# Key projection of the biased attention's first pair moved into the delta stage, and its bias turned through four PSUM banks around the norm

## The chip, the cores and the metric

The kernel runs on one core of a Trainium2 chip, in one launch. The metric is the device time of that launch in microseconds, the median of several runs. The engines are named as the profile names them: PE (matrix engine; PEld is its loading of weights), DVE (vector), ACT (scalar), POOL (GpSimd) and SP, which here only issues DMAs.

## The reference

Two batches of 256 tokens of width 256 go through six stages, each of which adds its result to x:

```
x = x + xattn_0(layernorm(x), ctx, ctx)            # 8 heads, 4096 context rows: "plain"
x = x + delta_rule(layernorm(x))                   # gated delta rule, chunks of 32: "delta"
x = x + experts(layernorm(x))                      # 15 experts, top 3, and a shared one
x = x + xattn_1(layernorm(x), ctx, ctx, bias)      # 16 heads, 4096 context rows: "biased"
x = x + quantised_attention(layernorm(x))
x = x + recurrent_cell(layernorm(x))
```

The biased attention is the stage whose beginning is changed:

```
k = split_heads(ctx @ Wk.T);  v = split_heads(ctx @ Wv.T);  q = split_heads(layernorm(x) @ Wq.T)
scores  = einsum('bhqd,bhkd->bhqk', q, k) * 256 ** -0.5 + bias      # bias is [256, 4096]
weights = softmax(scores);  out = merge_heads(weights @ v) @ Wp.T
```

Its keys depend on the context and a weight only, not on x. All is float32.

## The kernel before

Each stage is one block in which every engine has a program of its own, written out in order; semaphores join them, and the stages follow each other. `c.iterations`, `c.batches` and the semaphores of `c.attention` count on over the stages.

**Attention.** `cross_attention` works on pairs of heads, 8 pairs for each batch row in the biased stage, so 16 sweeps and the one ahead of them. Scores are held with the keys on partitions, in 16 tiles `kp` of 256 keys. While pair m is attended, the scores of pair m+1 are made, and the keys of pair m+2 and the values of pair m+1 are projected in pieces of 512 keys (`PIECES`). The first pair has no sweep ahead of it that could project its keys. At the head of the stage PE therefore runs `first_keys(g)` for eight groups `g` of 512 keys, each two float32 matmuls of 512 columns (line 320), through banks 4 to 7, and ACT copies each to `KT` (line 497).

**Bias.** It comes as queries by keys and has to be turned. `turn_bias(kp)` is four transposes into bank `kp % 3` (line 465), and DVE copies the bank back into `BIAS` (line 661). PE's order is: keys 0 and 1, the eight transposes of the normed x (line 128), a wait for their copy (`ln_ready`, DVE line 120), the queries (line 347), and then for g from 2 to 7 keys g and three `turn_bias`. The first scores (line 369) wait for the last copy.

**Norm.** DVE takes moments (lines 95, 98), ACT a square root (line 104), DVE the inverse and the normed rows (lines 110, 113), PE turns them (128), DVE copies them (120).

**Delta stage.** `delta_rule` projects q, k and v, convolves them on DVE, and turns them to rows in banks 2 to 7. DVE then rotates and normalises q and after it k (lines 1129 to 1146). ACT supplies the root of each (`norm_sums`, line 1027) and, ahead of the first one, scales v into `U` out of banks 6 and 7 (line 1023). PE turns q, k and k times beta (line 882), each as it becomes ready. Between these PE has nothing to do. The stage's small loads are twelve DMAs on SP's queue; ACT's line 1005 waits for all of them, and DVE's next work waits for ACT.

**Experts.** SP issues the weights of the first two experts, then for the biased stage its first pair's weights, four chunks of context and the bias, and then in a loop the weights of the other experts. ACT splits each weight into a high and POOL into a low part (lines 1342, 1446), from which PE multiplies (lines 1395, 1406).

Of the kernel before, what the change touches and what calls it, by code (L numbers as in the profile page):

```python
# [19 lines left out]
P = 128  # L20
# [4 lines left out]
T = B * S // P  # L25
# [135 lines left out]
def cross_attention(nc, c, k, tag, wqkv, w_out, b_out, ctx_t, biased, heads, scale):  # L161
# [16 lines left out]
    with ExitStack() as stack:  # L178
# [11 lines left out]
        KT = sb("keys", [P, S2])  # L190
# [26 lines left out]
        bias_turned, bias_kept = sem("bias_turned"), sem("bias_kept")  # L217
# [19 lines left out]
        def values_count(p, g):  # L237

            return piece_count(p - 1, ("V", g))

# [14 lines left out]
        with nc.Block() as block:  # L255
# [57 lines left out]
            def _(pe):  # L313
# [143 lines left out]
                def turn_bias(kp):  # L457
                    if kp == 0:
                        pe.wait_ge(rest_in, 16)
                    if kp >= 3:  # L460
                        pe.wait_ge(bias_kept, kp - 2)
                    for n in range(2):
                        for qt in range(2):
                            at = (2 * kp + n) * P
                            last = pe.transpose(c.ps[:, kp % 3, (2 * qt + n) * P:(2 * qt + n + 1) * P],
                                                BIAS[:, qt, at:at + P], c.ident[:, :])
                    last.then_inc(bias_turned, 1)

                first_keys(0)
                first_keys(1)  # L470
                norm_tensor(c, pe, k, bank=0)
                if b_out is not None:
                    pe.wait_ge(rest_in, 16)
                    pe.matmul(c.ps[:, 2, 0:D], c.ones[0:1, 0:P], bo[0:1, :], start=True, stop=True).then_inc(b_done, 1)
                pe.wait_ge(c.ln_ready, k + 1)
                queries(START)
                for g in range(2, NG):
                    first_keys(g)
                    if biased:
                        for kp in range(3 * (g - 2), min(3 * (g - 1), NP)):  # L480
                            turn_bias(kp)
                if b_out is not None:
                    pe.wait_ge(b_added, T)
                if biased:
                    pe.wait_ge(bias_kept, NP)
# [8 lines left out]
            def _(act):  # L494
# [56 lines left out]
                if b_out is not None:  # L551
                    act.dma_start(bo[:, :], b_out.rearrange("(o n) -> o n", o=1)).then_inc(rest_in, 16)
                norm_scalar(c, act, k)

                act.wait_ge(c.ln_std, k + 1)
                keys_out(NP * START + 1, 0, PIECE)
                keys_out(NP * START + 2, 1, PIECE + 1)
                queries_out(START)
                for g in range(2, NG):
                    keys_out(NP * START + g + 1, g, PIECE + g % 4)  # L560
# [7 lines left out]
            def _(dve):  # L568
# [89 lines left out]
                if biased:  # L658
                    for kp in range(NP):
                        dve.wait_ge(bias_turned, kp + 1)  # L660
                        dve.tensor_copy(BIAS[:, :, kp * 2 * P:(kp + 1) * 2 * P],
                                        c.ps[:, kp % 3, :].rearrange("p (t n) -> p t n", t=2)).then_inc(bias_kept, 1)
                    dve.wait_ge(bias_kept, NP)
# [1421 lines left out]
```

## Time and profile before

| | us |
|---|---|
| median of 3 runs | 2121.53 (2119.19 to 2121.89) |
| the profiled execution's own time | 2118.65 |
| its span in the trace | 2116.9 |
| PE busy | 1921.9 (91%) |
| DVE busy | 1637.3 (77%) |
| ACT busy | 830.5 (39%) |
| POOL busy | 928.8 (44%) |
| mean granted PE clock | 0.947 of full |

In the trace the plain attention ends at about 570 us, the delta stage at 746.5, the experts at 866, and the biased attention at about 1981. "PEclk" is the clock that the throttle granted PE: 1.00 is 2.4 GHz, 0.50 is 1.2 GHz. A timeline row gives start, length, engine, line, operation, names, count, and in brackets how long the engine idled before and what ended the idling. A row with a count is several instructions merged; a float32 matmul stands as two instructions, a transpose as one.

### The profile page before, as it was taken

Reading aid. Unit: us, or ns where it says so; the run is one execution under the profiler, and the core shown is the slowest. Engines: PE = TensorE matmul, PEld = TensorE weight load, DVE = VectorE, ACT = ScalarE, POOL = GpSimd, SP = SyncE. Lnnn points to the kernel's source line nnn. Section 1 sums busy time; section 2 is a strip of 40 time slices with the busy share of each in tenths; the row PEclk is TensorE's granted clock in tenths of the full one; section 3 lists DMA queues with packets and bytes.
Section 4 is the critical chain, followed back from the end, with each engine's and each line's share of the span. In section 5 each row is a group of like instructions: output and inputs, shape, how many; then the busy total and the mean of one; then the engine's idle time right before and its main releaser. Section 6 shows DMA issues by size and latency. Waiting matters only on the chain. (4 is left out here: it accounts for less than half of the span.)

```text
span 2116.9 us, 34534 instructions
## 1 busy us (share of the span) xinstructions
PE 1921.9 (91%) x12560; PEld 1317.8 (62%) x12562; DVE 1637.3 (77%) x2131; ACT 830.5 (39%) x1108; POOL 928.8 (44%) x438
## 2 busy tenths in 40 slices
PE   8999999999758889989999999999999999997526
PEld 5666666666338768656666666666666666664224
DVE  3576666767586356679999999999999999999562
ACT  3665655656330135223433334333343333434101
POOL 0454655546450034006555465554655546555100
PEclk9999999999869689999999999999999999999758
DMA  2000200000100063000000000110000000000001
GB/s 107 8 13 5 67 32 12 12 0 9 49 0 1 2 240 89 11 8 1 12 12 12 12 0 12 52 52 2 10 12 12 12 0 12 12 8 6 20 0 50
DMA packets 27717, 52.45 MB, mean 25 GB/s; under 512 B 4227, under 2 KB 15252, under 8 KB 27156
## 3 DMA queue, kind: packets, MB, share of 16 engines
q1 hardware_dynamic: 27200, 51.60, 7.5%
q8 instruction: 34, 0.56, 0.1%
q10 hardware_dynamic: 468, 0.16, 0.0%
q14 instruction: 15, 0.12, 0.0%
HBM read 51.23 MB, written 0.52 MB: 24 GB/s over the span
## 5 line engine op out<-in xcount | busy, mean ns | idle before, releaser
L298 POOL TENSOR_TENSOR biased_sums<-biased_sums,biased_scores 128x1024 f32<-128x1024 f32 x218 | 515.4, 2364 | 182.5 <-ACT biased_scores L524 165.7
L573 DVE TENSOR_TENSOR biased_scores<-ps,bias 128x1024 f32<-128x1024 f32 x256 | 311.7, 1218 | 51.8 <-PE ps L369 44.6
L587 DVE TENSOR_TENSOR ps<-ps,biased_scores 128x512 f32<-128x512 f32 x480 | 332.7, 693 | 4.1
L594 DVE TENSOR_TENSOR biased_scores<-biased_scores,ps 128x1024 f32<-128x1024 f32 x256 | 305.4, 1212 | 1.2 <-PE ps L409 1.2
L298 POOL TENSOR_TENSOR plain_sums<-plain_sums,plain_scores 128x1024 f32<-128x1024 f32 x106 | 250.5, 2363 | 80.9 <-ACT plain_scores L524 71.5
L329 PEld LDWEIGHTS ps<-weights_again,context_again 128*128 128x128 f32 x2048 | 239.6, 192 | 48.0 <-issue 34.0
L329 PE MATMUL ps<-weights_again,context_again 128*128 128x128 f32 x2048 | 262.0, 281 | 2.7 <-ACT biased_keys L497 1.4
L369 PE MATMUL ps<-biased_queries,biased_keys 64*128 64x256 f32 x2048 | 257.7, 390 | 5.9 <-DVE biased_scores L573 5.1
L524 ACT ACTIVATE biased_scores<-biased_scores 128x1024 f32<-128x1024 f32 x256 | 256.6, 1049 | 14.8 <-DVE biased_scores L594 13.8
L320 PE MATMUL ps<-context_again,weights_again 128*128 128x512 f32 x512 | 252.9, 617 | 4.8 <-PEq L1312 2.4
L587 DVE TENSOR_TENSOR ps<-ps,plain_scores 128x512 f32<-128x512 f32 x240 | 167.4, 698 | 115.5 <-ACT plain_scores L519 111.2
L381 PE MATMUL ps<-biased_scores,biased_values 128*64 128x256 f32 x2048 | 250.4, 386 | 1.9 <-ACT biased_scores L524 1.4
L369 PEld LDWEIGHTS ps<-biased_queries,biased_keys 64*128 64x128 f32 x2048 | 186.8, 186 | 62.4 <-issue 20.4
L497 ACT ACTIVATE biased_keys<-ps 128x512 f32<-128x512 f32 x128 | 76.5, 597 | 355.0 <-PE ps L320 355.0
L381 PEld LDWEIGHTS ps<-biased_scores,biased_values 128*64 128x64 f32 x2048 | 135.5, 136 | 123.5 <-issue 60.0
L508 ACT ACTIVATE biased_values<-ps 128x512 f32<-128x512 f32 x128 | 76.5, 598 | 310.5 <-PE ps L329 310.5
L298 POOL TENSOR_TENSOR biased_sums<-biased_scores 128x1024 f32<-128x1024 f32 x16 | 38.0, 2373 | 355.9 <-ACT biased_scores L524 355.9
L320 PEld LDWEIGHTS ps<-context_again,weights_again 128*128 128x128 f32 x512 | 88.6, 190 | 107.6 <-issue 92.4
L594 DVE TENSOR_TENSOR plain_scores<-plain_scores,ps 128x1024 f32<-128x1024 f32 x128 | 152.1, 1212 | 1.7 <-PE ps L409 1.7
L519 ACT ACTIVATE plain_scores<-ps 128x1024 f32<-128x1024 f32 x128 | 124.0, 1020 | 42.8 <-PE ps L369 42.7
L329 PEld LDWEIGHTS ps<-weights,context 128*128 128x128 f32 x1024 | 119.2, 191 | 29.1 <-issue 16.5
L329 PE MATMUL ps<-weights,context 128*128 128x128 f32 x1024 | 131.2, 281 | 4.7 <-ACT plain_values L508 3.4
(360 smaller groups left out, 2318.9 us busy)
## 6 DMA issues: line engine op xcount, KB each, us to landing
context<-in_ctx_t SPq DMA_DIRECT2D x8, 1024.0 KB, 5.3
moe_w<-in_moe_w SPq DMA_DIRECT2D x32, 256.0 KB, 2.8
context_again<-in_ctx_t SPq DMA_DIRECT2D x8, 1024.0 KB, 6.4
weights_again<-in_wqkv SPq DMA_DIRECT2D x45, 128.0 KB, 2.3
bias<-in_fside SPq DMA_DIRECT2D x1, 4096.0 KB, 22.2
biased_w_out<-in_w_out SPq DMA_DIRECT2D x16, 256.0 KB, 2.7
weights<-in_wqkv SPq DMA_DIRECT2D x21, 128.0 KB, 2.2
plain_w_out<-in_w_out SPq DMA_DIRECT2D x8, 256.0 KB, 2.8
```

The lines of the kernel that those rows point to most:

```text
L298: pool.tensor_tensor(both(SUM[:, :, :, :]), both((E[:, 0] if kp == 1 else SUM)[:, :, :, :]), both(E[:, kp, :, :, :]), ALU.add).then_inc(su ...
L320: last = pe.matmul(c.ps[:, bank, :], W[:, 1, i, :], CT[:, i, g * KG:(g + 1) * KG], start=(i == 0), stop=(i == DC - 1))
L329: last = pe.matmul(c.ps[:, PIECE, n * P:(n + 1) * P], CT[:, i, g * KG + n * P:g * KG + (n + 1) * P], W[:, 2, i, :], start=(i == 0), stop=( ...
L369: last = pe.matmul(out, KT[half, at:at + P], QS[half, :].rearrange("p (t j) -> p t j", t=2), start=True, stop=True)
L381: last = pe.matmul(c.ps[n * HD:(n + 1) * HD, OUT, h * S:(h + 1) * S], VS[:, 2 * kp + n, h * HD:(h + 1) * HD], E[:, kp, 2 * h:2 * h + 2, n, :],
L497: act.activation(KT[:, g * KG:(g + 1) * KG], c.ps[:, bank, :], ACT.Copy).then_inc(piece_kept, 1)
L508: act.activation(VS[:, 4 * g:4 * g + 4, :].rearrange("p a n -> p (a n)"), c.ps[:, PIECE, :], ACT.Copy).then_inc(piece_kept, 1)
L519: act.activation(both(E[:, kp, :, :, :]), scores_bank(kp), ACT.Copy).then_inc(scores_kept, 1)
L524: act.activation(at, at, ACT.Exp).then_inc(exp_done, 1)
L573: dve.tensor_tensor(E[:, kp, :, :, :].rearrange("p (h t) n j -> p h t (n j)", h=2), scores_bank(kp).rearrange("p (h t n) -> p h t n", h=2, ...
L587: ins = dve.tensor_tensor(to, highest, E[:, kp, :, n, :], ALU.max)
L594: dve.tensor_tensor(at, at, c.ps[:, LOWER, :].rearrange("p (a j) -> p a j", a=HQ).unsqueeze(2) .to_broadcast([P, HQ, 2, P]), ALU.add).then ...
```

## The change

The keys of the biased stage's first pair are no longer projected at its head. Their tile `keys_again`, the context and the weights get memory from the delta stage on, and SP issues their loads behind the delta stage's own twelve. PE projects groups 0 to 4 after the small matmul of gamma (line 875) and ahead of the transposes of q, and groups 5 to 7 between the transposes of q and of k, through banks 0, 6 and 7. ACT copies groups 0 to 2 after `U` and ahead of the first root, 3 and 4 after it, and 5 to 7 ahead of the second root. The experts' SP queue keeps only the bias. At the head of the biased stage `turn_bias` uses banks 4 to 7: three turns ahead of the norm's transposes, one after each of the four token tiles, two more before the wait for `ln_ready`, and seven after the queries. ACT copies eleven of the sixteen turned tiles and DVE five; two of ACT's stand ahead of the norm's square root.

```diff
-        KT = sb("keys", [P, S2])
+        KT = c.KT if biased else sb("keys", [P, S2])
...
-        bias_turned, bias_kept = sem("bias_turned"), sem("bias_kept")
+        bias_turned, bias_kept, bias_kept_dve = sem("bias_turned"), sem("bias_kept"), sem("bias_kept_dve")
+        DVE_TURNS = (6, 8, 10, 12, 14)
+        ACT_TURNS = tuple(kp for kp in range(NP) if kp not in DVE_TURNS)
+        TURN_BANK = 4
...
+        def turn_kept(kp):
+
+            if kp in DVE_TURNS:
+                return bias_kept_dve, DVE_TURNS.index(kp) + 1
+            return bias_kept, ACT_TURNS.index(kp) + 1
+
+        def turn_view(kp):
+
+            return c.ps[:, TURN_BANK + kp % 4, :].rearrange("p (t n) -> p t n", t=2)
+
+        def bias_view(kp):
+
+            return BIAS[:, :, kp * 2 * P:(kp + 1) * 2 * P]
...
                 def turn_bias(kp):
                     if kp == 0:
                         pe.wait_ge(rest_in, 16)
-                    if kp >= 3:
-                        pe.wait_ge(bias_kept, kp - 2)
+                    if kp >= 4:
+                        pe.wait_ge(*turn_kept(kp - 4))
                     for n in range(2):
                         for qt in range(2):
                             at = (2 * kp + n) * P
-                            last = pe.transpose(c.ps[:, kp % 3, (2 * qt + n) * P:(2 * qt + n + 1) * P],
+                            last = pe.transpose(c.ps[:, TURN_BANK + kp % 4, (2 * qt + n) * P:(2 * qt + n + 1) * P],
                                                 BIAS[:, qt, at:at + P], c.ident[:, :])
                     last.then_inc(bias_turned, 1)
 
-                first_keys(0)
-                first_keys(1)
-                norm_tensor(c, pe, k, bank=0)
-                if b_out is not None:
+                if biased:
+                    for kp in range(3):
+                        turn_bias(kp)
+                    for t in range(T):
+                        pe.wait_ge(c.ln_rows, T * k + t + 1)
+                        for j in range(DC):
+                            last = pe.transpose(c.ps[:, j, t * P:(t + 1) * P], c.XN[:, t, j * P:(j + 1) * P],
+                                                c.ident[:, :])
+                        if t == T - 1:
+                            last.then_inc(c.ln_turned, 1)
+                        turn_bias(3 + t)
+                    turn_bias(7)
+                    turn_bias(8)
+                    pe.wait_ge(c.ln_ready, k + 1)
+                    queries(START)
+                    for kp in range(9, NP):
+                        turn_bias(kp)
+                    pe.wait_ge(*turn_kept(NP - 2))
+                    pe.wait_ge(*turn_kept(NP - 1))
+                else:
+                    first_keys(0)
+                    first_keys(1)
+                    norm_tensor(c, pe, k, bank=0)
                     pe.wait_ge(rest_in, 16)
                     pe.matmul(c.ps[:, 2, 0:D], c.ones[0:1, 0:P], bo[0:1, :], start=True, stop=True).then_inc(b_done, 1)
-                pe.wait_ge(c.ln_ready, k + 1)
-                queries(START)
-                for g in range(2, NG):
-                    first_keys(g)
-                    if biased:
-                        for kp in range(3 * (g - 2), min(3 * (g - 1), NP)):
-                            turn_bias(kp)
-                if b_out is not None:
+                    pe.wait_ge(c.ln_ready, k + 1)
+                    queries(START)
+                    for g in range(2, NG):
+                        first_keys(g)
                     pe.wait_ge(b_added, T)
-                if biased:
-                    pe.wait_ge(bias_kept, NP)
 
...
+                def bias_out(kp):
+                    act.wait_ge(bias_turned, kp + 1)
+                    act.activation(bias_view(kp), turn_view(kp), ACT.Copy).then_inc(bias_kept, 1)
+
+                if biased:
+                    bias_out(0)
+                    bias_out(1)
+                    norm_scalar(c, act, k)
+                    for kp in ACT_TURNS[2:7]:
+                        bias_out(kp)
+                    queries_out(START)
+                    for kp in ACT_TURNS[7:]:
+                        bias_out(kp)
+                else:
                     act.dma_start(bo[:, :], b_out.rearrange("(o n) -> o n", o=1)).then_inc(rest_in, 16)
-                norm_scalar(c, act, k)
-
-                act.wait_ge(c.ln_std, k + 1)
-                keys_out(NP * START + 1, 0, PIECE)
-                keys_out(NP * START + 2, 1, PIECE + 1)
-                queries_out(START)
-                for g in range(2, NG):
-                    keys_out(NP * START + g + 1, g, PIECE + g % 4)
...
                 if biased:
-                    for kp in range(NP):
+                    for kp in DVE_TURNS:
                         dve.wait_ge(bias_turned, kp + 1)
-                        dve.tensor_copy(BIAS[:, :, kp * 2 * P:(kp + 1) * 2 * P],
-                                        c.ps[:, kp % 3, :].rearrange("p (t n) -> p t n", t=2)).then_inc(bias_kept, 1)
-                    dve.wait_ge(bias_kept, NP)
+                        dve.tensor_copy(bias_view(kp), turn_view(kp)).then_inc(bias_kept_dve, 1)
+                    dve.wait_ge(*turn_kept(NP - 2))
+                    dve.wait_ge(*turn_kept(NP - 1))
...
+        piece_done, piece_kept = c.attention["piece_done"], c.attention["piece_kept"]
+        KEY_PIECES, KEYS_BEFORE = 8, 16 * c.iterations
+        KG = S2 // KEY_PIECES
+
+        def key_bank(g):
+            return (0, 6, 7)[g % 3]
...
+                load_weights(c, sync, a["wqkv1"], 0)
+                load_context(c, sync, a["ctx_t"], 0)
...
+                def next_keys(g):
+                    if g == 0:
+                        pe.wait_ge(c.weights_in, 16 * (c.batches // B + 1))
+                        pe.wait_ge(gates_done, 2)
+                    elif g < 3:
+                        pe.wait_ge(v_ready, M)
+                    else:
+                        pe.wait_ge(piece_kept, KEYS_BEFORE + g - 2)
+                    if g % 2 == 0:
+                        pe.wait_ge(c.context_in[g // 2], 16 * c.batches + 16)
+                    for i in range(DC):
+                        last = pe.matmul(c.ps[:, key_bank(g), :], c.W[:, 1, i, :], c.CT[:, i, g * KG:(g + 1) * KG],
+                                         start=(i == 0), stop=(i == DC - 1))
+                    last.then_inc(piece_done, 1)
...
+                for g in range(5):
+                    next_keys(g)
                 pe.wait_ge(v_ready, M)
                 for s, (rows, ready) in enumerate([(Q, q_ready), (K, k_ready), (KB, k_ready)]):
+                    if s == 1:
+                        for g in range(5, KEY_PIECES):
+                            next_keys(g)
+                    if s == 2:
+                        pe.wait_ge(piece_kept, KEYS_BEFORE + KEY_PIECES)
                     pe.wait_ge(ready, max(s, 1))
...
+                def next_keys_out(g):
+                    act.wait_ge(piece_done, KEYS_BEFORE + g + 1)
+                    act.activation(c.KT[:, g * KG:(g + 1) * KG], c.ps[:, key_bank(g), :], ACT.Copy).then_inc(piece_kept, 1)
+
                 for s in range(2):
+                    for g in range(3) if s == 0 else range(5, KEY_PIECES):
+                        next_keys_out(g)
                     act.wait_ge(norm_sums, s + 1)
                     act.activation(NS[:, s, :], NQ[:, s, :], ACT.Sqrt).then_inc(norm_roots, 1)
+                    if s == 0:
+                        for g in range(3, 5):
+                            next_keys_out(g)
...
-                load_weights(c, sync, a["wqkv1"], 0)
-                load_context(c, sync, a["ctx_t"], 0)
                 load_bias(c, sync, a["fside"])
...
             if stage == 1:
                 first.close()
+                c.CT, c.W = c.sb("context_again", [P, DC, S2]), c.sb("weights_again", [P, 3, DC, P])
+                c.KT = c.sb("keys_again", [P, S2])
             if stage == 2:
-                c.CT, c.W = c.sb("context_again", [P, DC, S2]), c.sb("weights_again", [P, 3, DC, P])
                 c.BIAS = c.sb("bias", [P, 2, S2])
```

## Rows read from the trace of the kernel before

**Rows 1.** Busy time by stretch: length, busy us of each engine, granted PE clock, DMA share.

```profile
570.00:622.40 52.40, 23.58 (x83) 15.07 (x83) 44.34 (x80) 16.31 (x34) 27.51 (x22) 0.63 0.15 44
...
866.20:893.10 26.90, 24.67 (x108) 15.02 (x108) 14.70 (x30) 6.71 (x11) 0.00 (x0) 0.94 0.03 6
```

**Rows 2.** Timeline of the biased stage's start: start us, us, engine, line, names [idle before].

```profile
866.16 1.28 ACT L104 ACT_TABLE_LOAD   x1 [6.65 <-PEq L1312]
866.35 5.37 PE L320 MATMUL ps<-context_again,weights_again 128*128 128x512 f32 x8 [2.36 <-PEq L1312]
...
868.06 0.30 ACT L104 ACTIVATE deviation<-moments,eps 128x4 f32<-128x4 f32 x1 [0.61 <-DVE moments L98]
...
868.60 1.38 DVE L113 TENSOR_SCALAR XN<-X,moments,inverse 128x256 f32<-128x256 f32 x4
...
871.55 1.04 PE L128 MATMUL ps<-ident,XN 128*128 128x128 f32 x8
...
872.63 1.23 DVE L120 COPY XNT<-ps 128x1024 f32<-128x1024 f32 x1 [2.65 <-PE ps L128]
...
873.91 1.13 PE L347 MATMUL ps<-XNT,weights_again 128*128 128x256 f32 x4 [1.32 <-DVE XNT L120]
...
876.59 1.47 PE L465 MATMUL ps<-ident,bias 128*128 128x128 f32 x12
...
877.90 1.88 PE L320 MATMUL ps<-context_again,weights_again 128*128 128x512 f32 x4
...
891.74 0.60 PE L465 MATMUL ps<-ident,bias 128*128 128x128 f32 x4
...
891.94 0.60 ACT L497 ACTIVATE biased_keys<-ps 128x512 f32<-128x512 f32 x1 [2.43 <-PE ps L320]
...
892.38 0.69 DVE L661 COPY bias<-ps 128x512 f32<-128x512 f32 x1 [1.14 <-PE ps L465]
893.12 1.60 PEld L369 LDWEIGHTS ps<-biased_queries,biased_keys 64*128 64x128 f32 x16 [1.02 <-DVE bias L661]
```

**Rows 3.** Granted PE clock, in stretches around the start of that stage.

```profile
866.00:868.00 2.00, 1.65 (x3) 0.82 (x4) 1.77 (x8) 1.28 (x1) 0.00 (x0) 0.82 0.00 0
...
870.00:872.00 2.00, 2.00 (x9) 0.96 (x8) 0.00 (x0) 0.24 (x1) 0.00 (x0) 0.83 0.00 0
```

**Rows 4.** Timeline of the delta stage around its two gaps on PE.

```profile
581.13 0.20 ACT L1005 ACTIVATE delta_mix<-delta_mix 128x4 f32<-128x4 f32 x1 [7.47 <-DMA delta_mixer_norm<-in_L_attn_mixer_norm_w]
...
600.42 3.38 ACT L1023 ACTIVATE delta_u<-ps,delta_gates 128x64 f32<-128x64 f32 x16 [2.06 <-PE ps L871]
...
603.81 1.28 ACT L1027 ACT_TABLE_LOAD   x1
...
609.74 0.22 ACT L1027 ACTIVATE delta_norm_roots<-delta_norms 128x16 f32<-128x16 f32 x1 [4.64 <-DVE delta_norms L1143]
...
611.65 1.94 PE L882 MATMUL ps<-ident,delta_q 128*128 128x128 f32 x8 [10.95 <-DVE delta_q L1146]
...
622.38 1.97 PE L882 MATMUL ps<-ident,delta_k 128*128 128x128 f32 x8 [8.79 <-DVE delta_k L1146]
```

**Rows 5.** Busy time and granted clock of one stretch that holds only transposes on PE.

```profile
622.38:626.21 3.83, 3.82 (x16) 3.14 (x16) 1.67 (x6) 1.02 (x1) 0.00 (x0) 0.50 0.02 4
```

**Rows 6.** DMA issues of the experts' first 60 us: size, median us from issue to landing.

```profile
moe_w<-in_moe_w SPq DMA_DIRECT2D x16, 256.0 KB, 3.1
context_again<-in_ctx_t SPq DMA_DIRECT2D x4, 1024.0 KB, 10.6
```

**Rows 7.** Timeline of the experts' turn into their loop.

```profile
776.34 2.23 ACT L1342 ACTIVATE moe_w_parts<-moe_w 128x512 fp32r<-128x512 f32 x4 [6.40 <-DMA moe_w<-in_moe_w]
...
778.40 6.91 PEld L1395 LDWEIGHTS ps<-moe_x_parts,moe_w_parts 128*128 128x128 f32 x24 [0.33 <-POOL moe_w_parts L1446]
```

**Rows 8.** Steady sweeps: one stretch of 100 us, and the line that ends each sweep.

```profile
1100.00:1200.00 100.00, 99.57 (x664) 65.21 (x663) 95.02 (x109) 36.81 (x48) 56.94 (x25) 1.00 0.02 7
```

**Rows 9.** The instruction that ends each sweep: durations in ns, first and last start us.

```profile
L620 DVE TENSOR_TENSOR X<-ps,X x24: 684/684/693, 144.1 to 1980.2; 128x512 f32 x22, 128x512 f32<-128x512 f32 x2
```

More of the change, by code:

```diff
@@ L549, in sweep @@
                         exponential(m + 1, 3)
-                if b_out is not None:
-                    act.dma_start(bo[:, :], b_out.rearrange("(o n) -> o n", o=1)).then_inc(rest_in, 16)
-                norm_scalar(c, act, k)
-                act.wait_ge(c.ln_std, k + 1)
-                keys_out(NP * START + 1, 0, PIECE)
-                keys_out(NP * START + 2, 1, PIECE + 1)
-                queries_out(START)
-                for g in range(2, NG):
-                    keys_out(NP * START + g + 1, g, PIECE + g % 4)
+                def bias_out(kp):
[11 more added lines that the diff above has]
+                else:
+                    act.dma_start(bo[:, :], b_out.rearrange("(o n) -> o n", o=1)).then_inc(rest_in, 16)
+                    norm_scalar(c, act, k)
+                    act.wait_ge(c.ln_std, k + 1)
+                    keys_out(NP * START + 1, 0, PIECE)
+                    keys_out(NP * START + 2, 1, PIECE + 1)
+                    queries_out(START)
+                    for g in range(2, NG):
+                        keys_out(NP * START + g + 1, g, PIECE + g % 4)
                 sweep(START - 1, False, True, True)
```

## The prediction

> **What bounds the kernel now.** I read busy time by stretch first. From 1100 to 1200 us PE is busy 99.57 of 100 us at full clock and DVE 95.02 [rows 8]: the steady sweeps are PE's, and the change leaves their code alone. In the delta stage up to the transposes of k, DVE is busy 44.34 of 52.40 us and PE 23.58 [rows 1]. That stretch is DVE's, and PE's idle time costs nothing there. At the head of the biased stage PE is busy 24.67 of 26.90 us, DVE 14.70, ACT 6.71 [rows 1]: PE bounds it. The timeline says with what. From 866.35 to 893.12 no score is made, while keys and bias turns follow each other without a pause [rows 2]. Work taken off PE there is worth its full time, if it finds room in the delta stage.
>
> **The head of the biased stage.** Prices at full clock come from [rows 2]. Four transposes take 0.60 us and twelve 1.47, so one more costs 0.11 and the last has a tail of some 0.16; a `turn_bias` is 0.44. A key group is 1.88 less that tail, 1.72. The queries are 0.75 before the next work can go. At half clock all of it doubles. A copy of a turned bank costs ACT 0.60 (the same size as a key copy) and DVE 0.69.
>
> Eight key groups leave PE's queue, 13.8 us. Two of them filled PE's wait for the norm, so not all of it is gained; I lay out the new order instead. PE turns biases 0 to 2 from 866.35 to 867.7. ACT copies 0 and 1 until about 868.15, and only then comes the root. Its table load follows them: in the delta stage the load starts at 603.81, when the last copy of `U` ends (600.42 + 3.38), ahead of its own wait and behind the copies before it [rows 4]. So it no longer starts at 866.16 beside the moments but at 868.15, lasts 1.28 and lets the root go at 869.45 instead of 868.06 [rows 2]. That is 1.4 us late, and DVE's normed rows, PE's transposes and everything behind them wait for it. The first of the four rows is ready at 868.60 + 0.35 + 1.4 = 870.35.
>
> The ScalarE: Activation LUTs page of the Trainium skill (What ACT_TABLE_LOAD costs) adds a drain of about 1.38 us to each load; by it the root would be 2.8 us late, not 1.4, and the gain smaller by 1.4. The row here shows 1.28 us for the load, and since the root behind it waited for DVE it doesn't test the drain.
>
> From 870.4 PE has work without a pause: eight transposes, 13 turns, the queries. The clock decides its length. Before, it fell within 866 to 868 after PE's pause between the stages, and came back at about 870.7, 4.3 us after PE had restarted [rows 3]. I take the same here: half clock from 867.3, back at about 874.6. Three rounds of two transposes and a turn at half clock are 3 x 1.32, so the last row is turned at 870.4 + 3.96 + 0.44 = 874.8. DVE's copy (1.23 us) makes `ln_ready` true at about 876.1. Turns 6 to 8 fill exactly that (3 x 0.44). The queries end at 876.9, seven turns at 880.0, the tail and ACT's last copy at 880.8. ACT needs 0.60 for each second turn, that is, per 0.88 us of PE, and DVE 0.69: neither holds PE, and a bank is needed again only four turns later. Scores start at 880.85 instead of 893.12: **12.3 us gained**. Bounds: full clock all the way makes the 7.3 us of work end at 877.7 and scores start at 878.5, a gain of 14.6; a clock that comes back 3 us later costs 1.5, a gain of 10.8.
>
> **Gap 1 of the delta stage.** PE idled 10.95 us before the transposes of q at 611.65 [rows 4], so from 600.7. Five groups are 8.6 us at full clock and 17.2 at half. PE has been transposing since 598.4 and now goes on, so by the 4.3 us above the clock should be back by about 604.4. Group 0 then takes 3.4 us (to 604.15) and four groups at 1.72 end at 611.1, just before q is ready. ACT is the tighter one. It copies groups 0 to 2 after `U`, and the table load, hidden from 603.81 before, now stands behind them. Group 2 is done at 607.7, copied by 608.3, the load ends at 609.6, and the root is wanted at 609.74 [rows 4]. I book 0; there is 0.1 us to spare. Half clock throughout would end the copy at 611.65 and the load at 612.95: 3.2 us on DVE's chain.
>
> **Gap 2.** Three groups at full clock are 5.2 us from 612.8, done at 618.0, and the copies at 618.7; k is wanted by PE at 622.38. 3.7 us are spare, and I book 0. The pause that remains is long enough for the clock to fall again, so the work after it should run as before.
>
> **DMAs.** ACT waited until 581.13 for the last of the twelve small loads, and DVE for ACT [rows 4]. Now 4.4 MB follow them at once on the same queue. The nearest rows are the experts' first loads, which had such traffic behind them: sixteen took 3.1 us in the median, and context chunks 10.6 [rows 6]. If the small loads keep their place the delay is 0; if they end only with the context it is the 8 us or so that 4.4 MB need beyond it. I take 0.7, nearer to the first, since earlier issues are served earlier. The context itself is there long before 600.7. In the experts ACT no longer waits 6.40 us for weights behind 8 MB, but PE, which leads there, waited only 0.33 us for what follows [rows 7]: **0.3 gained**. The loads for the second pair stand behind `q_done` as before.
>
> **Sum.** -12.3 + 0.7 - 0.3 = -11.9 us against the profiled execution's own time of 2118.65 (span 2116.9), that is 2106.8. The median of the runs shown lies 2.9 higher, so I forecast 2121.53 - 11.9 = **2109.6 us**.
>
> **Rivals.**
>
> *The clock stays at half while PE only transposes (18 in 100).* A stretch with nothing but transposes, 3.83 us with PE busy all the time, ran at 0.50 from end to end [rows 5], though steady matmuls brought the clock back in about that time [rows 3]. After the change the head of the stage is nearly all transposes; before, key groups stood between them. Then the last row is turned at 874.9, XNT copied at 876.3, turns 6 to 8 end at 877.6, the queries at 879.1, seven turns at 885.3, scores start at 886.1: 7.0 gained, and some 2 us given back because the first scores also start at half clock. With the other terms that is a gain of 4.6, 2117 us. Against it stands that 3.83 us may just be too short. The TensorE: Matmul & The Clock Gate page of the Trainium skill (Part 4: PE-mode transpose) says that transposes don't count as busy for the clock; by it this rival would be the forecast.
>
> *The projection doesn't fit the delta stage (7 in 100).* Either the clock stays low in gap 1 (3.2 us late), or the small loads end with the context (8 us late). The gain shrinks to 4 to 9 us: 2113 to 2117.
>
> *Slower: the steady sweeps get longer (5 in 100).* `keys_again` and the tiles around it move in memory, and 17 sweeps from 893 to 1980 us read them, 64 us each [rows 9]. With PE at 99.57 in 100 [rows 8] any slower read of keys shows in full. It decides from (12.3 + 4.2) / 17 = 1.0 us a sweep, 1.5%; at 1.5 us a sweep the time is 2135. Nothing in the trace speaks for it; the instructions are the same.
>
> *Forecast (70 in 100).* Its own range is 2105 to 2112: 14.6 or 10.8 at the head, 0 to 2 for the loads, and 1 us for the runs' spread.
>
> **Range and chances.** 2104 to 2117.5 takes in the first two rivals and leaves out the slower one and the ends. A measurement here can tell 0.2%, 4.2 us, from no change, so faster means below 2117.3. The forecast, nearly all of the second rival and over half of the first lie there: 0.87. Within 0.2%: 0.08. Slower: 0.05.
>
> **What the changed profile would show.** At the head: the root at about 869.5 less any shift, no row of line 320 before the first scores, scores some 14.5 us after the stage's start instead of 27, a granted clock back at 1.00 by 875. In the delta stage: PE busy through both gaps, the first root within 0.3 us of where it was, transposes of k at 622.4 to 623.1. The sum is wrong if the table load shows up as DVE idle time ahead of line 1145, if line 1005 starts over 2 us late, or if PEclk reads 0.50 until the scores.

## Result

The changed kernel takes 2108.93 us (median of 5 runs, 2107.53 to 2111.48) against 2120.06 before (5 runs): ratio 0.9949, 95% interval 0.9935 to 0.9962, 11 us faster. In a second set of 6 runs it took 2113.54 against 2119.05, ratio 0.9969 (0.9957 to 0.9980), 6 us faster. The later sets ran on a chip each, so kernels are compared within a set. Both intervals lie below 1; the first is clear of 0.2%, the second ends at it. The two sets disagree on the size, 11 or 6 us. Of the 29 runs of the kernel before in one later set, with a median of 2119.95 in the tables below, four were disturbed (2199.65 to 10448.1 us) and don't enter the ratios, which are also estimated from the single runs and so can differ a little from the quotient of two medians. The forecast was 2109.6 with a range of 2104 to 2117.5.

The profiled execution of the changed kernel has a span of 2107.1 us, 9.8 less than before. The head of the biased stage, in its timeline:

```profile
868.50 1.50 PE L482 MATMUL ps<-ident,bias 128*128 128x128 f32 x12 [2.21 <-PEq L1393]
869.17 1.09 ACT L583 ACTIVATE bias<-ps 128x512 f32<-128x512 f32 x2 [7.34 <-PE ps L482]
...
870.27 1.28 ACT L104 ACT_TABLE_LOAD   x1
871.57 0.30 ACT L104 ACTIVATE deviation<-moments,eps 128x4 f32<-128x4 f32 x1
...
872.11 1.38 DVE L113 TENSOR_SCALAR XN<-X,moments,inverse 128x256 f32<-128x256 f32 x4
872.58 0.44 PE L492 MATMUL ps<-ident,XN 128*128 128x128 f32 x2 [2.57 <-DVE XN L113]
...
876.30 1.13 PE L364 MATMUL ps<-XNT,weights_again 128*128 128x256 f32 x4
877.26 3.22 PE L482 MATMUL ps<-ident,bias 128*128 128x128 f32 x28
...
880.52 0.60 ACT L583 ACTIVATE bias<-ps 128x512 f32<-128x512 f32 x1 [0.28 <-PE ps L482]
881.22 2.00 PE L386 MATMUL ps<-biased_queries,keys_again 64*128 64x256 f32 x16 [0.73 <-DVE bias L703]
```

From the first PE row to the first scores it is 12.7 us, against 26.8 in [rows 2]. No key group is left. The table load stands behind ACT's two copies, and the root 3.1 us behind the stage's start (1.9 before). After that PE's rows follow each other. The first scores wait for both copying engines; the bracket names DVE, but its last copy ended at 880.78 and ACT's only at 881.12 (880.52 + 0.60). The granted clock (third number from the end) never fell here:

```profile
868.00:870.00 2.00, 1.50 (x12) 1.29 (x12) 1.64 (x6) 0.83 (x2) 0.00 (x0) 1.00 0.03 8
870.00:872.00 2.00, 0.01 (x1) 0.00 (x0) 0.42 (x5) 1.97 (x4) 0.00 (x0) 1.00 0.00 0
872.00:874.00 2.00, 1.42 (x13) 1.43 (x14) 1.45 (x5) 0.86 (x2) 0.00 (x0) 1.00 0.00 0
```

The delta stage, in its timeline:

```profile
583.83 0.20 ACT L1077 ACTIVATE delta_mix<-delta_mix 128x4 f32<-128x4 f32 x1 [10.28 <-DMA delta_mixer_norm<-in_L_attn_mixer_norm_w]
...
603.19 2.81 PE L913 MATMUL ps<-context_again,weights_again 128*128 128x512 f32 x4
...
606.55 7.13 PE L913 MATMUL ps<-context_again,weights_again 128*128 128x512 f32 x16 [0.55 <-ACT delta_u L1095]
...
610.90 1.28 ACT L1105 ACT_TABLE_LOAD   x1
...
612.45 0.22 ACT L1105 ACTIVATE delta_norm_roots<-delta_norms 128x16 f32<-128x16 f32 x1 [0.27 <-DVE delta_norms L1224]
...
614.36 1.07 PE L954 MATMUL ps<-ident,delta_q 128*128 128x128 f32 x8 [0.68 <-DVE delta_q L1227]
...
615.26 5.32 PE L913 MATMUL ps<-context_again,weights_again 128*128 128x512 f32 x12
...
625.09 1.71 PE L954 MATMUL ps<-ident,delta_k 128*128 128x128 f32 x8 [4.52 <-DVE delta_k L1227]
```

From line 1077 to the root it is 28.62 us, from there to the transposes of k 12.64; in [rows 4] 28.61 and 12.64. Eight key groups have gone into the two gaps and delay nothing. The table load ended 0.27 us before the root was wanted. But line 1077 itself is 13.73 us behind the stage's first DVE row (570.10), against 10.92 before.

The two traces side by side, each part from its first DVE row to the next part's. "Rest of delta" runs from the transposes of k to the experts.

| us | before | changed | difference |
|---|---|---|---|
| delta: start to the small loads' landing | 10.92 | 13.73 | +2.81 |
| delta: both gaps | 41.25 | 41.26 | 0.0 |
| rest of delta | 124.53 | 123.01 | -1.52 |
| experts | 119.29 | 120.40 | +1.11 |
| biased: start to first scores | 26.92 | 12.72 | -14.20 |
| biased: 17 sweeps | 1088.10 | 1087.12 | -0.98 |
| quantised attention | 87.34 | 87.06 | -0.28 |
| recurrent cell, to the end | 48.34 | 51.70 | +3.36 |

With the start, 0.11 us earlier, the sum is -9.8. The span is printed to 0.1 us, so the last row is good to 0.1 us only. Three rows are large: the head, the loads, and the last stage, whose code is the same in both kernels. The rows "rest of delta" and "experts" can't be put down to the change: a second profile of the changed kernel has 128.46 and 119.19 us there, one of the kernel before 128.74 and 119.38. The last stage's beginning and its end before, with the busy time and granted clock of its stretches:

```profile
2076.07 11.99 PE L1921 MATMUL ps<-XNT,cell_w 128*128 128x512 f32 x24 [2.67 <-DMA cell_b<-in_cell_b]
...
2104.91 5.41 PE L1944 MATMUL ps<-cell_state,cell_u 128*128 128x256 f32 x16 [3.05 <-DVE cell_state L1983]
...
2068.50:2080.00 11.50, 5.90 (x14) 3.41 (x15) 5.00 (x15) 0.30 (x1) 0.00 (x0) 0.54 0.50 184
2080.00:2090.00 10.00, 10.00 (x29) 5.29 (x28) 0.00 (x0) 0.13 (x1) 0.00 (x0) 1.00 0.00 0
...
2100.00:2110.00 10.00, 6.95 (x25) 5.43 (x23) 1.99 (x3) 2.36 (x5) 0.00 (x0) 0.83 0.00 0
2110.00:2117.00 7.00, 1.41 (x10) 0.86 (x8) 1.42 (x4) 0.69 (x1) 0.00 (x0) 0.97 0.22 75
```

and in the changed kernel:

```profile
2063.77 13.26 PE L2000 MATMUL ps<-XNT,cell_w 128*128 128x512 f32 x24 [3.53 <-DMA cell_b<-in_cell_b]
...
2093.87 6.72 PE L2023 MATMUL ps<-cell_state,cell_u 128*128 128x256 f32 x16 [3.05 <-DVE cell_state L2062]
...
2055.40:2067.00 11.60, 5.20 (x12) 3.05 (x13) 4.99 (x15) 0.30 (x1) 0.00 (x0) 0.50 0.49 182
2067.00:2077.00 10.00, 10.00 (x22) 4.35 (x21) 0.00 (x0) 0.00 (x0) 0.00 (x0) 0.89 0.00 0
...
2087.00:2097.00 10.00, 6.95 (x25) 5.55 (x24) 1.98 (x3) 2.51 (x6) 0.00 (x0) 0.81 0.00 0
2097.00:2107.10 10.10, 4.68 (x18) 3.41 (x16) 1.42 (x4) 1.37 (x2) 0.00 (x0) 0.84 0.15 52
```

PE waits 0.86 us longer for the last small load; the projection and the last product take 1.3 us more each, at a lower clock. By the shares of these stretches the clock rose about 10.5 us behind the stage's start before (0.54 over 11.50 us) and about 13.8 in the changed kernel (0.50 over 11.60 us, then 0.89 over 10.00). In the last two stretches the clock was low for some 3.8 us before (0.83 and 0.97) and 7.0 in the changed kernel (0.81 and 0.84).

### The profile page after: what moved, and what is told of

Its sections match the earlier page's. It is cut to its first block and busy times, and to the rows that moved or that the text cites. A ratio compares the mean times of both kernels' runs of the same rounds, so it can differ in the third digit from the quotient of the medians.

```text
span 2107.1 us, 34539 instructions
## 1 busy us (share of the span) xinstructions
PE 1923.3 (91%) x12562; PEld 1317.6 (63%) x12562; DVE 1630.1 (77%) x2120; ACT 837.1 (40%) x1119; POOL 928.7 (44%) x438
## 5 line engine op out<-in xcount | busy, mean ns | idle before, releaser
L386 PE MATMUL ps<-biased_queries,keys_again 64*128 64x256 f32 x2048 | 257.3, 390 | 6.8 <-DVE biased_scores L615 6.0
L337 PE MATMUL ps<-context_again,weights_again 128*128 128x512 f32 x480 | 236.2, 614 | 2.4 <-DMA context_again<-in_ctx_t 1.7
L386 PEld LDWEIGHTS ps<-biased_queries,keys_again 64*128 64x128 f32 x2048 | 186.9, 186 | 63.0 <-issue 20.4
L527 ACT ACTIVATE keys_again<-ps 128x512 f32<-128x512 f32 x120 | 71.7, 597 | 338.6 <-PE ps L337 338.6
L337 PEld LDWEIGHTS ps<-context_again,weights_again 128*128 128x128 f32 x480 | 82.4, 189 | 99.5 <-issue 84.3
```

Source lines behind the costliest of these rows:

```text
L337: last = pe.matmul(c.ps[:, bank, :], W[:, 1, i, :], CT[:, i, g * KG:(g + 1) * KG], start=(i == 0), stop=(i == DC - 1))
L386: last = pe.matmul(out, KT[half, at:at + P], QS[half, :].rearrange("p (t j) -> p t j", t=2), start=True, stop=True)
L527: act.activation(KT[:, g * KG:(g + 1) * KG], c.ps[:, bank, :], ACT.Copy).then_inc(piece_kept, 1)
```

## Experiments

Times are medians; each set of runs has its own runs of the kernel before beside it.

| kernel | us | before beside it | ratio (95%) |
|---|---|---|---|
| loads_only | 2120.20 | 2119.95 | 0.9999 (0.9989 to 1.0010) |
| keys_only | 2115.60 | 2119.95 | 0.9980 (0.9969 to 0.9990) |
| bias_only | 2123.45 | 2119.95 | 1.0015 (1.0005 to 1.0025) |
| context_waits | 2110.50 | 2119.95 | 0.9960 (0.9946 to 0.9973) |
| changed, again | 2113.54 | 2119.05 | 0.9969 (0.9957 to 0.9980) |
| root_first | 2112.08 | 2119.05 | 0.9965 (0.9955 to 0.9976) |
| both | 2110.27 | 2119.05 | 0.9960 (0.9945 to 0.9974) |
| turns_last | 2115.22 | 2119.05 | 0.9978 (0.9967 to 0.9990) |
| before, again | 2119.54 | 2120.01 | 0.9997 (0.9988 to 1.0007) |
| before_cell | 2116.84 | 2120.01 | 0.9988 (0.9979 to 0.9997) |
| cell_early | 2105.43 | 2120.01 | 0.9936 (0.9923 to 0.9950) |
| both_cell | 2104.68 | 2120.01 | 0.9942 (0.9928 to 0.9955) |

Single runs of one kernel spread over 4 to 12 us, so edits worth 1 to 3 us are read from the stages of the profiles. From those of all kernels:

| us | start to loads landed | rest of delta | experts | head | sweeps | last stage |
|---|---|---|---|---|---|---|
| before | 10.92 | 124.53 | 119.29 | 26.92 | 1088.10 | 48.34 |
| before, again | 10.65 | 128.74 | 119.38 | 26.93 | 1088.12 | 48.40 |
| loads_only | 13.90 | 124.55 | 119.20 | 26.92 | 1087.93 | 46.61 |
| keys_only | 13.51 | 124.55 | 119.24 | 19.57 | 1087.35 | 47.26 |
| bias_only | 10.73 | 128.36 | 119.11 | 28.36 | 1087.17 | 51.78 |
| changed | 13.73 | 123.01 | 120.40 | 12.72 | 1087.12 | 51.70 |
| changed, again | 12.58 | 128.46 | 119.19 | 14.62 | 1087.27 | 51.66 |
| context_waits | 10.42 | 124.59 | 119.19 | 14.62 | 1087.13 | 51.80 |
| root_first | 12.72 | 126.58 | 119.13 | 13.64 | 1088.13 | 51.29 |
| both | 11.11 | 124.52 | 119.23 | 13.68 | 1087.88 | 51.86 |
| turns_last | 12.87 | 126.73 | 121.60 | 17.62 | 1088.08 | 51.74 |
| before_cell | 11.02 | 124.27 | 119.29 | 26.92 | 1088.00 | 45.86 |
| cell_early | 15.11 | 122.99 | 120.50 | 12.71 | 1087.08 | 45.96 |
| both_cell | 10.84 | 124.49 | 119.44 | 13.64 | 1087.80 | 45.91 |

**The loads alone moved** (loads_only).

```diff
             def _(sync):     # delta stage, behind its twelve loads
+                load_weights(c, sync, a["wqkv1"], 0)
+                load_context(c, sync, a["ctx_t"], 0)
...
             def _(sync):     # experts
-                load_weights(c, sync, a["wqkv1"], 0)
-                load_context(c, sync, a["ctx_t"], 0)
```

> The kernel before with one edit: the weights and the context of the biased stage are loaded behind the delta stage's twelve loads instead of in the experts; the projection and the bias turning stay where they were. Theory 'traffic behind' (the 4.4 MB that follow the small loads hold them back): ACT's root of the rotation mix (line 1005) starts 13.7 to 13.8 us after the stage's first DVE row as in the changed kernel, against 10.9 before, and the time is 1 to 3 us above before. Theory 'chance' (the late landing in the one profile of the changed kernel was an accident of issue times): 10.9 to 11.3 us and a time within 1 us of before. Both expect the head of the biased stage to stay at 26.8 us from its first PE row to the first scores.

```profile
585.20 0.20 ACT L1007 ACTIVATE delta_mix<-delta_mix 128x4 f32<-128x4 f32 x1 [10.45 <-DMA delta_mixer_norm<-in_L_attn_mixer_norm_w]
```

13.90 us behind the stage's start at 571.30. Nothing but the loads and the place of their tiles in memory has moved, so "traffic behind" holds for the landing. Its 3 us don't show in the time, which is that of before within its interval of 2 us either way; in this profile the last stage is 1.7 us shorter than in that of before, and the cause of that isn't shown.

**Context issued after the small loads** (context_waits).

```diff
+                sync.wait_ge(loads, 16 * 10)
                 load_weights(c, sync, a["wqkv1"], 0)
                 load_context(c, sync, a["ctx_t"], 0)
```

> The changed kernel with one wait added on SP: the weights and the context are issued only after the delta stage's small loads have landed. Theory 'traffic behind': line 1077 starts 10.9 to 11.1 us after the stage's first DVE row instead of 13.7, and the time falls 2 to 3 us below the changed kernel, to about 2106; the context still lands some 16 us after it is issued, by 598, ahead of its first use at 600. Theory 'chance': 10.9 to 11.1 us as well in most runs but the time is that of the changed kernel within 1 us. A third way: the context now lands late, key group 0 waits for it, and the time rises.

```profile
582.45 0.20 ACT L1078 ACTIVATE delta_mix<-delta_mix 128x4 f32<-128x4 f32 x1 [6.97 <-DMA delta_mixer_norm<-in_L_attn_mixer_norm_w]
...
600.83 1.94 PE L914 MATMUL ps<-context_again,weights_again 128*128 128x512 f32 x4
```

10.42 us, and key group 0 starts without a wait for the context. The time doesn't show the 2 to 3 us that were expected: its ratio of 0.9960 lies between the two of the changed kernel, 0.9949 and 0.9969. Over all profiles the landing comes at 12.58 to 15.11 us (seven with traffic behind, mean 13.5) against 10.42 to 11.11 (seven without, mean 10.8): 2.7 us, and the two groups don't touch.

**Each half of the change by itself** (keys_only, bias_only).

```diff
# keys_only, against the changed kernel
-        DVE_TURNS = (6, 8, 10, 12, 14)
+        DVE_TURNS = tuple(range(NP))
...
-        TURN_BANK = 4
+        TURN_BANK = 0
...
+                    norm_tensor(c, pe, k, bank=0)
                     pe.wait_ge(c.ln_ready, k + 1)
                     queries(START)
-                    for kp in range(9, NP):
+                    for kp in range(NP):
                         turn_bias(kp)
...
# bias_only, against the changed kernel: next_keys is gone, the loads are back in the experts
-                    for kp in range(9, NP):
-                        turn_bias(kp)
+                    for g in range(NG):
+                        if g >= 3:
+                            pe.wait_ge(piece_kept, NP * START + g - 2)
+                        keys(START, g, g % 3)
+                        if 9 + g < NP:
+                            turn_bias(9 + g)
```

> The changed kernel with its projection in the delta stage, but the bias turned as before: three banks, all sixteen copies on DVE, all turns behind the queries, the norm's root first. Theory 'PE's 13.8 us of keys are the gain': the head shrinks from 26.8 us to about 17 (5.7 us to the end of the norm's copy, the queries, sixteen DVE copies at 0.63 us), some 7 us faster than before in time, so the rest of the change is worth 4 to 5 us. Theory 'the way the bias is turned is the gain': the head stays above 22 us and the time within 3 us of before.

> The changed kernel with its four banks, two copying engines and turns around the norm, but the eight key groups back at the head of the biased stage behind the queries, and nothing moved into the delta stage. Theory 'PE's 13.8 us of keys are the gain': the head is 12.7 + 13.8 = 26.5 us, the time within 1.5 us of before. Theory 'the way the bias is turned is the gain': the head is under 22 us and the time 5 us or more below before. If the two parts simply add, this run and the keys-only run together give the whole gain; I expect them not to, since before the keys filled PE's wait for the norm, which turns fill here.

The projection moved by itself shortens the head by 7.4 us, the bias turning by itself lengthens it by 1.4. Together they give 12.3 to 14.2, so they don't add. Both heads are longer than expected, 19.57 us against about 17 and 28.36 against 26.5. For bias_only the clock accounts for it: the 26.5 were 12.7 + 13.8, with the clock up, and with 14.62 us, the head of the changed kernel at a low clock, the sum is 28.4. In keys_only DVE sets the pace of the turns:

```profile
879.80 8.64 DVE L686 COPY bias<-ps 128x512 f32<-128x512 f32 x14 [0.16 <-PE ps L482]
...
888.54 2.00 PE L386 MATMUL ps<-biased_queries,keys_again 64*128 64x256 f32 x16 [1.19 <-DVE bias L686]
```

Fourteen of its copies follow each other without a pause, 0.62 us each, where PE needs 0.44 for a turn at full clock. The new turning removes that pace and fills PE's wait for the norm, which the keys filled before; that is worth 5 to 7 us, but only once the keys are gone. In bias_only PE has as much to do as before, and the later root is paid. The kernel is also some 3 us slower than before (1.0015), not within 1.5 us: the last stage takes 51.78 us, as in every kernel with the new turning in which PE starts late there (51.3 to 51.9), against 47.26 in keys_only. So of the 5 to 7 us that the new turning is worth at the head, 4.4 are lost again there, and the times of keys_only and of the changed kernel, 0.9980 and 0.9969 in two sets, can't be told apart.

**The root ahead of the first two copies** (root_first), beside the changed kernel again.

```diff
-                    bias_out(0)
-                    bias_out(1)
                     norm_scalar(c, act, k)
+                    bias_out(0)
+                    bias_out(1)
```

> The changed kernel with the norm's square root ahead of ACT's first two bias copies, so that its table load runs beside DVE's moments again. Theory 'the late table load costs the head': the root starts 1.86 us after the stage's first DVE row instead of 3.07, the rows, PE's transposes and the first scores come 1.2 us earlier (head 11.5 us instead of 12.7), the time falls by 1.2 us. Rival 'the copies behind it become the bound': the first turned banks are copied later, PE waits for a bank at turns 4 to 6, and the head stays at 12.5 us or more.

> The changed kernel once more, on the chip and in the rounds of the three others, as their base. Both theories of the head expect a second profile with the first scores 12.5 to 15 us after the stage's first PE row: 12.7 if the clock stays up as in the first profile, up to 14.5 if it falls. The loads: 13.7 us from the stage's first DVE row to line 1077 if the traffic behind them is the cause, 10.9 if the first profile was an accident.

The head of the changed kernel again ("changed, again" is the run called after_again):

```profile
874.31 1.67 PE L482 MATMUL ps<-ident,bias 128*128 128x128 f32 x12 [2.21 <-PEq L1393]
...
878.86 1.06 PE L482 MATMUL ps<-ident,bias 128*128 128x128 f32 x4
...
888.93 2.00 PE L386 MATMUL ps<-biased_queries,keys_again 64*128 64x256 f32 x16 [0.73 <-DVE bias L703]
```

A turn of four takes 1.06 us here and 0.60 in the first profile: this time the clock fell, and the head is 14.62 us. So is that of context_waits. root_first and both have the same low clock and 13.64 and 13.68: the root's place is worth 1.0 us, not 1.2. The copies behind it don't become the bound: in root_first PE's rows follow each other from its restart 2.87 us behind the stage's start (4.07 in the changed kernel again) to the end of its turns at 12.90. In time root_first is 1.5 us below the changed kernel beside it, which the intervals can't tell from nothing. The loads landed at 12.58 us in the changed kernel again, less than the 13.7 expected and more than in any profile without traffic behind them.

**Both edits** (both).

> The changed kernel with both edits: the context is issued after the small loads have landed, and the norm's root stands ahead of the bias copies. If both single costs are what I take them for, the gains add: 2.8 + 1.2 = 4 us below the changed kernel, about 2105 us. If the clock's chance decides more than either, the time is within 1 us of the changed kernel.

The stages show both gains (11.11 and 13.68). In time, 3.3 us below the changed kernel beside it, with intervals that overlap: inconclusive as a time.

**Nothing but transposes** (turns_last).

```diff
-                    for kp in range(3):
+                    norm_tensor(c, pe, k, bank=0)
+                    pe.wait_ge(c.ln_ready, k + 1)
+                    for kp in range(NP):
                         turn_bias(kp)
...
                     queries(START)
-                    for kp in range(9, NP):
-                        turn_bias(kp)
```

> The changed kernel, but at the head of the biased stage PE first idles for the norm, then turns the normed x, waits for its copy, turns all sixteen biases without a matmul between them, and only then makes the queries. It asks whether a stretch of nothing but transposes brings PE's clock back. Theory 'transposes count as work': the clock falls during the norm and is back at 1.00 about 4 us into the turns; the turns take 7 to 9 us, the head 14 to 17 us. Theory 'transposes don't count': 0.50 to the end of the turns, which take 14 us, and the head is 21 us or more; the first scores run at half clock too.

Busy time by stretch, with the granted clock as the third number from the end:

```profile
878.90:884.60 5.70, 5.70 (x27) 5.70 (x28) 0.00 (x0) 3.38 (x6) 0.00 (x0) 0.50 0.00 0
884.60:889.00 4.40, 4.40 (x40) 4.37 (x40) 3.35 (x5) 2.73 (x6) 0.00 (x0) 1.00 0.00 0
```

Until the queries at 888.66 these are transposes only. PE did nothing else from 875.5 on, and the clock rose at 884.6 in the middle of the turns: 0.21 us each before, 0.11 after. Transposes count as work. The stretch of [rows 5], 3.83 us long, ended before that. The clock came back 5.8 us into the turns, later than the 4 expected, so the turns took 10.04 us and the head 17.62, both somewhat beyond what "transposes count as work" gave (7 to 9 and 14 to 17) and far from the 14 and 21 or more of the other theory.

**The early start of the last stage** (cell_early, before_cell, both_cell). PE waits for the projection's weight alone; ACT, DVE and the recurrence wait for the other two loads.

```diff
-                sync.dma_start(W[:, :, :, :], a["cell_w"]).then_inc(loads, 16)
+                sync.dma_start(W[:, :, :, :], a["cell_w"]).then_inc(w_in, 16)
...
-                pe.wait_ge(loads, 16 * 3)
+                pe.wait_ge(w_in, 16)
                 for gate in (FG, IG, CG):
```

> The changed kernel with one edit in the last stage, which the change leaves alone: PE starts the cell's input projection when its weight has landed instead of when all three loads of the stage have. In the profiles so far this stage took 46.6 to 48.3 us in the kernels with the old bias turning and 51.3 to 51.9 in those with the new one. Theory 'late start and clock': the last small load lands 0.6 to 0.9 us later there, PE starts too late for the clock to rise at the first chance, and the stage pays 3 to 5 us; with the early start PE is busy from the end of the norm, and the stage takes 45 to 48 us, so that the time falls by 3 to 5 us. Rival 'it is something else in that stage': it stays above 50 us and the time is that of the changed kernel.

> The kernel before with the same early start in the last stage. It tells whether the stage's length is evened out: under 'late start and clock' it takes within 1 us of what it takes in the changed kernel with the early start, the gain here is only 0 to 2 us, and the two kernels with the early start lie 10 to 12 us apart. Under the rival the two stay as far apart as before and after are.

> The changed kernel with all three edits: the context issued after the delta stage's small loads have landed, the norm's root ahead of the bias copies, and the early start in the last stage. If each is worth what its run or profile shows (2.4, 1.0 and 3 to 5 us), the time is 6 to 8 us below the changed kernel, about 2104 us, and this is the fastest of all.

> The kernel before once more, for a second profile. Both theories of the loads expect line 1005 at 10.7 to 11.1 us after the stage's first DVE row, and of the head 26.8 us. The last stage is the question: 46.6 to 48.3 us again if it belongs to this kernel, above 51 if it is chance from run to run.

In cell_early the two rows of the stage read:

```profile
2066.79 12.68 PE L2001 MATMUL ps<-XNT,cell_w 128*128 128x512 f32 x24 [1.32 <-DVE XNT L120]
...
2096.32 3.72 PE L2026 MATMUL ps<-cell_state,cell_u 128*128 128x256 f32 x16 [3.06 <-DVE cell_state L2065]
```

PE starts when the normed x is there, and the last product takes 3.72 us, not 6.72. The stage takes 45.86, 45.96 and 45.91 us in the three kernels with the edit: the difference of 3.36 us is gone. The kernel before gains 2.5 us by it in the profile, somewhat more than the 0 to 2 expected, the changed one 5.7. Its ratio lies just below 1 (0.9988, 0.9979 to 0.9997), and cell_early's 0.9936 lies below both ratios of the changed kernel. The two kernels with the early start are 2116.84 and 2105.43 us, 11.4 apart, as "late start and clock" asked. The kernel before, profiled once more (before_again), has 48.40 us in the last stage, 10.65 to the landing and 26.93 at the head, so its shorter last stage is no chance of one profile. both_cell is the fastest median, 2104.68, but can't be told from cell_early; that the loads and the root add to it stands on the stages alone (10.84 and 13.64, span 2100.7 against 2106.6).

## Why the prediction was right

The forecast of -11.9 us is close to the first measurement (-11.1) and more than double the second (-5.5). What moves, what it is worth at the head and that the gaps have room for it came out as written; that the time fits so well is in part luck, since a mis-sized term and a missing one were met by a better clock at the head. Term by term:

- **The head, 12.3 us gained (10.8 to 14.6).** Right, and its working too: with the clock low, as assumed, two profiles have 14.62 us to the first scores where I had 14.5, a gain of 12.3. With the clock up, 12.72 where I had 12.15. That it would fall was my choice from one trace; it fell in one of two profiles of this kernel. Of the seven profiles with the projection moved and the new turning around the norm it fell in five and stayed up in two (the first of the changed kernel and cell_early).
- **The late root, 1.4 us.** The root came 1.2 us late in the profile (3.07 against 1.86 behind the stage's start). root_first gives 1.0 of it back. The root started 0.02 us after the load's 1.28, so the further 1.38 us that the ScalarE: Activation LUTs page of the Trainium skill (What ACT_TABLE_LOAD costs) adds as a drain are not there in this case. The trace of the kernel before would have told: a table load starts at 946.74, lasts 1.28, and the next ACTIVATE starts at 948.03.
- **The gaps, 0.** Right in every profile of the projection: 28.6 to 28.7 and 12.6 us as before, with 0.27 us to spare at the table load, where I had 0.1.
- **The small loads, 0.7 us.** Mis-sized: 2.7. The prediction named line 1005 over 2 us late as a sign that its sum is wrong, and in the changed profile it is 2.81 late (line 1077 there): this term of the sum is the one that failed. I took the row of the experts' weights [rows 6] as nearest, but only four of those sixteen loads were issued ahead of the context; the other twelve came after it. DVE's chain starts with this wait, so it is paid in full.
- **The experts, 0.3 gained.** Not seen: 119.11 to 119.38 us in the four profiles in which nothing was moved out of them, 119.13 to 119.44 in seven of those with the loads moved, and 120.40 to 121.60 in the other three.
- **The last stage.** No term of the sum stood for it, and it costs 3.4 us. The change's gain is 14.2 or 12.3 at the head, less 2.7 for the loads and 3.4 here: 6 to 8 us, plus up to 1 in the sweeps. The first profile came out near the forecast partly because the head's better clock (2 us) stood against these costs. With the last stage evened out, the change is worth 11.4 us (before_cell against cell_early), in whose profile the head had the better clock too.
- **Half clock through the turns.** Refuted by turns_last; so is the rule of the TensorE: Matmul & The Clock Gate page of the Trainium skill (Part 4: PE-mode transpose) that transposes don't count as busy, for these float32 transposes, which the trace lists as MATMUL; whether they ran in the mode that the page means isn't shown.
- **The projection doesn't fit.** Its half about the gaps is refuted. Its half about the loads was right in kind, at 2.7 us instead of 8.
- **Longer sweeps.** Refuted: 1087.1 to 1088.1 us for the 17 sweeps in every kernel.

**What stays open** is why the last stage's loads land later. Its state is copied when they have landed, 7.2 to 7.6 us after the stage's start in the five profiles with the old turning of the bias, 8.0 to 8.4 in the nine with the new. That is a clean split, but the stage's own code is the same; what carries it there wasn't found. The traces narrow it down: from issue to landing the last of the three loads takes 6.6 to 7.0 us in the five and 7.2 to 7.5 in the nine, the first 4.8 to 5.2 and 5.4 to 5.8, while the second takes 6.7 to 6.9 in all. So the transfers themselves take longer. Some 0.3 us of the 0.86 are not the landing: in the changed kernel DVE's first row comes 0.06 us after the first issue, in the kernel before 0.36, which lengthens the last stage in the table and shortens the quantised one (-0.28). The early start shows only that the lateness was the cost. "Rest of delta" differs by 4.2 us between two profiles of the kernel before (124.53 and 128.74) and by 5.8 over all profiles; that much of the spread of the single times comes from it is likely, not shown.

## What to carry to other kernels

Work that doesn't depend on the running result goes into the gaps of a stage that another engine bounds, and two halves of such a change need not add: the second is worth something only where it removes the next bound. Loads put right behind a stage's own small loads hold those back; one wait on the issuing queue avoids it. And it pays to compare the stages that a change doesn't touch: a gain can be given back there, and the median of the whole doesn't say where.

## What the runs showed of the hardware

- Traffic on the same queue behind small loads delayed them by 2.7 us in the mean of seven profiles each, though they had been issued first (13.5 against 10.8 us from the stage's first DVE row).
- A start of PE 0.86 us later in the last stage went with a stage 3.4 us longer: the clock rose about 13.8 us behind its start instead of 10.5, and the last product took 6.72 us instead of 5.41. Starting PE earlier on work already there took all of it back and 2.5 us more.
- An ACTIVATE that waited for nothing else started 0.01 to 0.02 us after a table load of 1.28 us had ended, and the load stood behind the copies ahead of it and ahead of its own instruction's wait.
- Transposes alone brought the clock back: 0.50 until 884.6, then 1.00, with nothing else on PE since 875.5.
